# Router logits out of the normalised rows and the head outputs, in column strips, instead of out of the new rows

## The reference

```python
# x (4, 2048, 512); ctx (4, 77, 384); 16 heads of 32; 8 experts, top 2, 1024 slots each
q = layernorm(x) @ Wq + bq;  k = ctx @ Wk + bk;  v = ctx @ Wv + bv
x = x + softmax(clip(q k^T / sqrt(32))) v @ Wo + bo
n = layernorm(x)
dot = n @ expert_embeddings.T                    # the logits, (8192, 8)
weights = softmax over the top 2 of dot          # the others are 0
ones = (weights > 0); keep those whose running count per expert is <= 1024
tokens = the kept rows of n, per expert          # (8, 1024, 512)
out = relu(tokens @ first_linear[e].T) @ second_linear[e].T
final = x + scatter_add(out * weight)
```

## Time and profile before

| | |
|---|---|
| median of 3 runs | 1450.96 us |
| the profiled execution | 1453.71 us |
| its span, first to last instruction | 1451.9 us |
| busy: TensorE matmul | 1318.1 us (91%) |
| VectorE | 990.7 us (68%) |
| ScalarE | 811.4 us (56%) |
| GpSimd | 718.6 us (49%) |
| granted TensorE clock, mean | 0.96 of full |

### The profile page before, as it was taken

One profiled execution on the slowest core, in us unless ns is written; L12 is line 12 of the kernel. 1 busy time (PEld: TensorE's weight loads), 2 busy tenths in 40 slices (PEclk: granted clock), 3 DMA queues, 4 the chain that ended last, 5 costly groups with the idle time before them and its releaser, 6 DMA issues.

```text
span 1451.9 us, 30528 instructions
## 1 busy us (share of the span) xinstructions
PE 1318.1 (91%) x12267; PEld 778.8 (54%) x12330; DVE 990.7 (68%) x1808; ACT 811.4 (56%) x1336; POOL 718.6 (49%) x717
## 2 busy tenths in 40 slices
PE   7648999988999899998648999999999999999996
PEld 3436777766676666765436444444444444444442
DVE  8768898999989997899875545455454545455421
ACT  4558888866998889987455504334251413334110
POOL 3287878775778678876413333241513224241301
PEclk9869999999999999999878999999999999999998
DMA  6147898966898767787514665655646465564401
GB/s 195 52 104 184 207 247 213 235 175 169 182 225 192 186 153 188 169 227 175 158 56 141 182 162 159 160 152 128 190 115 178 143 152 176 146 146 120 106 15 44
DMA packets 319575, 228.89 MB, mean 158 GB/s; under 512 B 253305, under 2 KB 253689, under 8 KB 319434
## 3 DMA queue, kind: packets, MB, share of 16 engines
q1 hardware_dynamic: 304074, 176.28, 48.8%
q0 software_dynamic: 15360, 50.66, 12.0%
HBM read 118.98 MB, written 50.86 MB: 117 GB/s over the span
## 4 chain that ended last, share of the span: by engine, by line
PE 70%; DVE 13%; POOL 6%; issue 4%; ACT 3%; SPq 2%; DMA 1%; DVEq 0%; POOLq 0%; ACTq 0%
PE ps L1213 23%; PE ps L1199 23%; PE ps L1099 8%; PE ps L1029 6%; PE ps L1080 3%; PE ps L1116 2%; POOL sd L542 2%; PE ps L1013 2%; DVE ps L1435 1%; DVE sm L1464 1%; DVE x L1486 1%; PE ps L1052 1%; POOL ph L548 1%; PE ps L1002 1%; POOL qT L524 1%
## 5 line engine op out<-in xcount | busy, mean ns | idle before, releaser
L1199 PE MATMUL ps<-xT,w1s 128*128 128x512 f16 (+1 forms) x1632 | 336.0, 368 | 1.9 <-DVE xT L1729 1.5
L1213 PE MATMUL ps<-w2s,hT 128*128 128x512 f16 x1536 | 332.8, 379 | 0.0
L849 ACT ACTIVATE hT<-ps 128x512 f16<-128x512 f32 (+1 forms) x136 | 77.8, 572 | 355.7 <-PE ps L1199 355.7
L1199 PEld LDWEIGHTS ps<-xT,w1s 128*128 128x128 f16 x1632 | 160.5, 98 | 175.2 <-issue 1.9
L1213 PEld LDWEIGHTS ps<-w2s,hT 128*128 128x128 f16 x1536 | 150.2, 98 | 181.3
L593 POOL DMA_INDIRECT out_dram<-ys,idx x64 | 71.4, 1116 | 278.7 <-DVE ys L1769 274.5
L542 POOL TENSOR_TENSOR sd<-sd,rr 128x1232 f32<-128x1232 f32 x64 | 144.2, 2253 | 125.3 <-ACT rr L750 125.3
L1029 PE MATMUL ps<-xnT,wqh 128*128 128x256 f16 x1536 | 196.7, 280 | 5.5 <-ACT partq L732 5.3
L1099 PE MATMUL ps<-woh,oT 128*128 128x512 f16 x768 | 183.4, 389 | 9.6 <-POOL oT L530 3.8
L1759 DVE SCALAR_TENSOR_TENSOR hT<-ps,hT 128x512 f16<-128x512 f32 (+1 forms) x136 | 88.6, 658 | 138.1 <-ACT hT L849 138.0
L1769 DVE SCALAR_TENSOR_TENSOR ys<-ps,gs,og 128x512 f32<-128x512 f32 x64 | 48.0, 751 | 189.7 <-PE ps L1213 189.7
(11 more groups left out here) (206 smaller groups left out, 2003.3 us busy)
## 6 DMA issues: line engine op xcount, KB each, us to landing
xr<-x SPq DMA_DIRECT2D x64, 256.0 KB, 3.7
xrow_dram<-x SPq DMA_DIRECT2D x64, 256.0 KB, 3.6
out_dram<-x SPq DMA_DIRECT2D x64, 256.0 KB, 4.3
stage<-w1T SPq DMA_DIRECT2D x8, 2048.0 KB, 9.6
stage<-w2T SPq DMA_DIRECT2D x8, 2048.0 KB, 8.5
xt<-x SPq DMA_DIRECT2D x59, 256.0 KB, 3.3
xs<-x SPq DMA_DIRECT2D x56, 256.0 KB, 4.1
wqf<-wq SPq DMA_DIRECT2D x1, 1024.0 KB, 7.0
```

The costliest lines, as they stand in the source:

```text
L1199: ins = pe.matmul(hb[z][:, 0:wide], w1s[e % 2][:, a, k, ic * P:(ic + 1) * P], xT[:, 4 * b + k, cols], start=(k == 0 and i == 0), stop=(k = ...
L1213: ins = pe.matmul(yb[z][:, :], hT[:, a, k, s * P:(s + 1) * P], w2s[e % 2][:, b, k, :], start=(k == 0 and i == 0), stop=(k == 7 and i == 2))
```

## The change

The new row is x1 = x + co * (oT Wo + ...) + bo, so its logits are a sum of three parts: the logits of x, those of the head outputs, and a constant. The first part comes from the normalised rows `xnT` times the expert columns, divided by the row's first norm. (The row's mean drops out, since the expert columns are centred.) The second comes from `oT` times Wo times the expert columns, a 512 by 8 matrix that is made once (`expert_mm`, from a turned copy of Wo that is loaded beside it). Both sets of expert columns are split in hi and lo, side by side in 16 of 32 columns.

- **TensorE**: `t2` and `logits` are gone. New are `xe_mm(G)` and `oe_mm(G)`, once per pair of tiles each: 32 fp16 products, with 32 expert columns as the weights in one column strip of the array, and 64 columns (32 rows of each of the two tiles) that move. The eight products of a strip stand one after the other, then the next strip's. `xe_mm` stands between the first `q_mm` and `pv_mm` in even iterations, `oe_mm` before `o_mm` in odd ones. Ahead of the loop the sum over the expert columns moves in front of `q_mm(0, 0)`; `xe_mm(0)` and `expert_mm` are new.
- **VectorE**: `xe_out` and `oe_out` turn the 128 by 64 result in blocks of 32 by 32, from PSUM to SBUF, once per pair each. `routing` loses its copy, runs the norm's three operations first, then the six operations of `logits(R)` in four steps. Ahead of the loop: a maximum and a scale of the expert columns, their split, and (at h = -5) that of the product with Wo.
- **ScalarE**: `t2_copy` is gone (64 copies of 128 by 512).
- **GpSimd**: a third `all_max`, of the expert columns, between the second and the third `q_lo` of pair 0, and two memsets.
- **SyncE**: the expert columns are loaded earlier; a turned Wo (1 MB) and bo are loaded after Wo.
- `pick`, `put`, `lg` and others lie in other places in SBUF.

```diff
@@ gpsimd, ahead of the loop
+            pool.memset(exs[:, :, :], 0.0)
+            pool.memset(ews[:, :, :], 0.0)
...
             all_max(0, 1)
             all_max(1, 2)
             q_lo(0, 0)
             q_lo(0, 1)
+            all_max(8, 3)
             q_lo(0, 2)
             q_lo(0, 3)
@@ scalar
-                act.wait_ge(S["t2"], t + 1)
-                act.copy(x1T[:, :, :].rearrange("p k n -> p (k n)"), bT[:, :]).then_inc(S["x1T"], 1)
@@ tensor
-                for k in range(4):
-                    ins = pe.transpose(bT[:, k * P:(k + 1) * P], x1[:, t % XO, k * P:(k + 1) * P], identf[:, :])
...
-                for k in range(4):
-                    ins = pe.matmul(bM[:, E * j:E * (j + 1)], x1T[:, k, :], embc[:, k, :], start=(k == 0),
-                                    stop=(k == 3))
...
+            def strips(out, w, src):
+                for i in range(4):
+                    for k in range(4):
+                        for a in range(2):
+                            rows = src(a, k).rearrange("p (j n) -> p j n", j=TG)[:, :, DH * i:DH * (i + 1)]
+                            ins = pe.matmul(out[DH * i:DH * (i + 1), :], w[:, k, :], rows,
+                                            start=(k == 0 and a == 0), stop=(k == 3 and a == 1),
+                                            tile_position=(0, DH * i))
+                return ins
+            def xe_mm(G):
+                pe.wait_ge(S["xTl"], TG * G + TG)
+                if free["M"]:
+                    pe.wait_ge(*free["M"])
+                strips(bM[:, 0:64], exs, lambda a, k: xnT[:, G % 2, 4 * a + k, :]).then_inc(S["xm"], 1)
+            def oe_mm(G):
+                pe.wait_ge(S["olo"], 2 * G + 2)
+                if free["M"]:
+                    pe.wait_ge(*free["M"])
+                strips(bM[:, 64:128], ews, lambda a, g: oT[:, G % 2, a, g, :]).then_inc(S["om"], 1)
+            def expert_mm():
+                for g in range(4):
+                    for k in range(4):
+                        pe.matmul(bM[:, 320 + E * g:320 + E * (g + 1)], wot[:, k, g * P:(g + 1) * P], embc[:, k, :],
+                                  start=(k == 0), stop=(k == 3))
@@ the loop of tensor
+                if half == 1:
+                    oe_mm(G)
                 o_mm(h)
                 if H:
                     invert(H)
                 tx(h + 11)
                 q_mm(Q, 2 * part)
+                if part == 1:
+                    xe_mm(Q)
                 pv_mm(G + 1, half)
                 s_mm(h + 7)
-                t2(h)
                 q_mm(Q, 2 * part + 1)
-                logits(h)
+                if h == -6:
+                    expert_mm()
@@ vector
+            def xe_out(G):
+                    dve.wait_ge(S["xm"], G + 1)
+                    dve.transpose(xe[:, t:t + TG, :].rearrange("p j c -> p (j c)"), bM[:, 0:64]).then_inc(S["xe"], 1)
+            def logits(R):
+                then(dve.reciprocal(den[:, 0:n], rs1[:, t0:t1]))
+                then(dve.tensor_tensor(lg[:, 0:n, :], mine[0][:, :, 0:E], mine[0][:, :, E:2 * E], ALU.add))
+                yield
+                then(dve.tensor_tensor(m8[:, 0:n, :], mine[1][:, :, 0:E], mine[1][:, :, E:2 * E], ALU.add))
...
+                k = then(dve.tensor_tensor(lg[:, 0:n, :], lg[:, 0:n, :],
+                                           den[:, 0:n].unsqueeze(2).to_broadcast([P, n, E]), ALU.mult))
+                yield
...
+                k = then(dve.scalar_tensor_tensor(lg[:, 0:n, :], m8[:, 0:n, :], scr[:, 37:38], lg[:, 0:n, :],
+                                                  ALU.mult, ALU.add))
+                yield
...
+                then(dve.tensor_tensor(lg[:, 0:n, :], lg[:, 0:n, :], be[:, :].unsqueeze(1).to_broadcast([P, n, E]),
+                                       ALU.add))
+                yield
             def routing(R):
-                dve.wait_ge(S["lg"], t1)
-                dve.tensor_copy(lg[:, 0:n, :], bM[:, 0:n * E].rearrange("p (j e) -> p j e", j=n)
-                                ).then_inc(S["lgc"], 1)
-                yield
+                yield from second_norms(R)
+                yield from logits(R)
@@ the loop of vector (the same in the last iterations for oe_out)
                 residual(h)
+                if h % 2:
+                    oe_out(h // 2)
...
+                if h % 2 == 0:
+                    xe_out((h + 9) // 2)
```

More of the change, by code:

```diff
@@ L82, in alternate, with xattn_moe @@
                 gens.remove(gen)
-def xattn_moe(nc, x, ctxT, wq, bq, wk, bk, wv, bv, wo, bo, embT, w1T, w2T, out, xrow):
+def xattn_moe(nc, x, ctxT, wq, bq, wk, bk, wv, bv, wo, bo, woT, boT, embT, w1T, w2T, out, xrow):
     ctx = ExitStack()
@@ L200, in xattn_moe @@
         vsh = sb("vsh", [P, 2, B, D], F16)
+        pick = sb("pick", [P, 4, TG, 2, P], F16)
+        put = sb("put", [P, 4, TG, 2, 64], F16)
+        oe = sb("oe", [P, 16, 32], F32)
+        assert place[0] <= early1
         place[0] = oT_at
@@ L626, in gpsimd @@
                 if h == -7:
-                    all_max(3, 3)
+                    all_max(3, 4)
                 if h == -6:
-                    all_max(2, 4)
+                    all_max(2, 5)
                 if h == -3:
@@ L1014, in t2 @@
-                ins.then_inc(S["t2"], 1)
-                free["T"] = S["x1T"], t + 1
+                    ins = pe.matmul(bM[:, 352:360], bob[:, k:k + 1].to_broadcast([P, P]), embc[:, k, :],
+                                    start=(k == 0), stop=(k == 3))
+                ins.then_inc(S["ew"], 1)
+                free["M"] = S["ewl"], 2
             def q_mm(G, g):
@@ L1226, in tensor @@
             values_mm(1)
-            q_mm(0, 0)
-            q_mm(0, 1)
             pe.wait_ge(S["l_em"], 16)
@@ L1233, in tensor @@
             ins.then_inc(S["early"], 1)
+            q_mm(0, 0)
+            q_mm(0, 1)
             q_mm(0, 2)
@@ L1237, in tensor @@
             tx(2)
+            xe_mm(0)
             values_mm(3)
@@ L1260, in tensor @@
                 pv_mm(G + 1, half, 1)
+                if half == 1:
+                    oe_mm(G)
                 o_mm(h)
                 s_mm(h + 7)
-                if h > TAIL:
-                    logits(h - 1)
                 if H:
                     invert(H)
-                t2(h)
                 if h == 59:
@@ L1277, in tensor @@
                     rank(3)
-            logits(T - 1)
             invert([24, 25, 26])
@@ L2015, in layout @@
         "bo": c(g["L0_xattn_bo"]),
+        "woT": c(g["L0_xattn_Wo"].reshape(4, 4, DH, D).transpose(3, 1, 0, 2).reshape(D, D)),
+        "boT": c(g["L0_xattn_bo"].reshape(4, P).T),
         "embT": c(g["L0_ffn_expert_embeddings"].T),
```

152 lines of the change are left out of this document (91 added, 61 removed).

## The result

The changed kernel takes 1480.74 us in the median (1477.84 to 1482.75, four runs), the kernel before, run beside it, 1451.61 (1449.02 to 1458.66, four runs). The ratio is 1.0194, with a 95% interval of 1.0169 to 1.0220. I had forecast 1455 and at most 1468. The direction was right; the size, 4 us, was not: the profiled executions differ by 25.2 us (spans 1451.9 and 1477.1).

What follows compares the result with a forecast made beforehand. TensorE was taken to set the pace in calm stretches, VectorE in the routing tiles. Relief -8, VectorE +6, head +7 and last tiles -1.5, with a rounded half for bank M, gave +4: 1455 us, range 1443 to 1468.

Steps and rivals of the forecast that it cites:

- Head, +7.0: Ahead of the loop: the fourth `q_lo` ends 7.0 us later, with no slack behind it; bounds 0 to 8.
- the detour: GpSimd ahead of the loop: `all_max(8)` between `q_lo`s adds one change of code each way, about 6 us.
- Products, 0.030: TensorE's new 64-column products: 0.030 us each as in `invert`, 1.92 us per pair, weight loads hidden.
- the rival's estimate of 0.06: TensorE's weight loads don't hide: 0.06 us per new product, a pair loses 1.4 us, 1487 us in all; chance 0.08.
- TensorE's relief, -8: Calm tiles: TensorE sets the pace, each pair gains 0.54 us; 17.5 pairs give -9.4, taken as -8 us.
- VectorE, +6: VectorE in the loop: block transposes +4 and the new logits operations +2, together +6 us.
- the turnings, +4: VectorE's block transposes from PSUM, 0.2 us per tile: nothing in calm tiles, +4 us in 24 routing tiles.
- the sum of 11: Six `logits(R)` operations on VectorE: 3.7 us per large span, 11 us for three, before deductions.
- 4.4 for `dd`: VectorE's `dd` moves three steps back, behind its waits for GpSimd: 2.2 us off in each of two spans.
- The +2 of this sub-sum: VectorE's logits operations: 11, less 1 for the copy, 3.5 for the third span and 4.4 for `dd`.
- Waits on bank M, half a microsecond: A rounded half microsecond added to the sum for what stands behind the new waits on bank M.
- Last tiles, -1.5: Last four tiles: -3.5 us without `t2`, +1.1 for `oe_mm(31)`, +0.8 for the last span's routing.

Runs made afterwards that it cites:

- Both edits together: Changed kernel with `all_max(8)` directly behind `all_max(1)` and the eight expert-column mean products behind `q_mm(0, 1)`: 1470.94 us, ratio 1.0141.
- the two runs: Kernel before without `t2`, its copy and most of `logits`: 1439.94 us; changed kernel with 4 of 32 products per `xe_mm` and `oe_mm`: 1470.67 us.
- the step ahead of `s_recip`: Changed kernel with five `logits(R)` operations in one step before `s_recip`, the `oe` sum earlier as one reduction: 1467.99 us, ratio 1.0092.
- mended: Changed kernel with five logits operations before `s_recip`, `all_max(8)` and mean products moved, last `oe_mm` and its turning before `rank(3)`: 1461.95 us, ratio 1.0056.

## Why the forecast was right in sign and wrong in size

Two steps failed: the relief on TensorE, booked one for one, and the price of the routing steps on VectorE, put at +2 and measured at 16.7. Both errors made the change look cheaper than it was; the right sign rests on the head's 7 us.

- **Head, +7.0: right in size** (7.8), and the steps named are there: `q_lo(0, 2)` at 45.61 behind 6.77 us of "issue", switches of 5.90 and 6.77. Both edits together take 6.2 of the 7.7 away. But the detour, to which I gave 6 of the 7 us, gave back only 2.2 when it went alone, in a profile with a dip of the clock; so the number is borne out and its split is not. Profiles of one head differ by up to 4 us, which I had not in the range.
- **Products, 0.030: cheaper**, 0.023 and 0.020, and their loads hide. Of the rival's estimate of 0.06, which the Trainium skill's rule (TensorE: Matmul & The Clock Gate, Part 3) would give for strips that share their rows, this case shows nothing.
- **TensorE's relief, -8: the first step that failed.** I read 97.5% busy as "sets the pace" and booked the relief one for one. Measured: 0.16 per microsecond in the calm tiles. An estimate from the two runs, over all 64 tiles: the removal returns 13.1, the new products take 8.6 of it again (7.5 for 28 of 32), which leaves -4.5 where I had -8. The changed kernel's calm tiles 0 to 16 gained nothing at all (+0.4).
- **VectorE, +6: the step that failed most.** Its parts: the turnings, +4, were worth about 0.7 (doubled). The six operations I had priced at 3.7 us per span; they took 5.5. From the sum of 11 I took off 3.5 because the third span's would be absorbed, and 4.4 for `dd`. The third span's first tiles lost 3.6 like the others. `dd` and the subtraction ahead of it took 10.0 us with their waits before (5.7 + 2.5 + 1.8) and 9.2 after (5.2 + 3.8 + 0.2): 0.8 and not 4.4. The +2 of this sub-sum was measured at 16.7, by leaving five of the operations out with three of their steps. The operations' own time is 16.6 us in the three large spans, the copy that went 0.8; the turning of `xe` and TensorE's `oe_mm` stand behind them. But that the two numbers agree is not the whole account. From tile 16 to 63 VectorE's operations other than turnings take 457.8 us before, 470.5 in the changed kernel and 456.5 with the step ahead of `s_recip`, and this last one still loses 7.5 us there. So held operations explain about half of the 16.3, and the other half is not traced to a cause.
- **Waits on bank M, half a microsecond: undersized.** `oe_mm` sat idle 17.4 us ahead of its products and `xe_mm` 9.9; taking 9.7 of it away gave 7 from tile 16 to 63, part of which is the same time as in the point before.
- **Last tiles, -1.5: half right.** Tiles 60 to 62 gain 3.4 us. Tile 63 loses 4.2 and not 1.1: `oe_mm(31)` waits 2.12 us for bank M until `ranking(3)` has read it, and it and the `o_mm` behind it run at a lower clock (0.50 granted from 757 to 761 us). That `o_mm` takes 4.87 us, against 3.92 in the kernel before and 2.75 at full clock. TensorE's timeline:

```profile
757.76 1.22 PE L1013 MATMUL ps<-oT,ews 128*32 128x64 f16 x32 [2.12 <-DVE pm L1691]
758.92 0.61 PE L1135 MATMUL ps<-bo,onesb 128*128 128x512 bf16 x1
759.32 4.87 PE L1140 MATMUL ps<-woh,oT 128*128 128x512 f16 x12
```

What stays open: why mended still loses some 10 us between tiles 35 and 57, operation by operation; what the half of the loop's loss is that stays when VectorE's operations take no longer in all than before; and whether a schedule exists in which none of VectorE's routing steps meets GpSimd's long ones. That the shift from one held operation to another explains it was seen in rows, not shown by a run.

## What to carry to other kernels

An engine that is busy 97% of a stretch need not set its pace: before booking relief, take the work out once and see what a microsecond returns (here 0.16). Price a small operation by where it stands, not by its mean: the same addition took 0.23 or 2.25 us, and which depends on what the neighbour engine has just begun; moving it moves everything behind it too. When a new result shares a bank, a queue or a semaphore with old work, list who stands behind it at each of its turns, the last one above all.

## What the runs showed of the hardware

- Some VectorE operations on SBUF operands that start while GpSimd works on a large fp32 tensor end only with GpSimd's: 2.25 us for 128 elements, 2.47 for 16 (`dd`). This was not only so with two inputs, as my expectations had it: `TENSOR_SCALAR` on 16 int32 took 1.55 and 0.16. Others never were held: in the changed kernel the view of single lines gives the shortest, median and longest of each (ns),

```profile
L1491 DVE TENSOR_REDUCE sm<-sd x128: 744/782/789, 72.9 to 724.9; 128x8 f32<-128x616 f32 x128
...
L1519 DVE BATCH_NORM_STATS2 st6b<-x x64: 650/680/696, 132.8 to 765.1; 128x6 f32<-128x512 f32 x64
...
L1621 DVE MAX8 m<-lg x64: 128/150/170, 299.1 to 771.6; 128x8 f32<-128x8 f32 x64
...
L1557 DVE STREAM_TRANSPOSE xe<-ps x32: 216/228/241, 43.1 to 687.4; 128x64 f32<-128x64 f32 x32
```

  so in this kernel the reduction of one input, the statistics, `MAX8` and the block transpose out of PSUM were never the longer for standing beside GpSimd.
- 64-column products in one column strip after another: 0.020 to 0.023 us each; strips taking turns: 0.010. The weight loads hid in both: a quarter of a 256-column product of `q_mm`, 0.109 us in the earlier trace rows, is 0.027.
- GpSimd's change between a reduction and ordinary work cost 5.87 to 7.75 us all six times between 31 and 76 us of the changed kernel, in either direction, and not only the first.
- Two profiles of the same program up to that point had granted clocks of 0.89 and 1.00 between 20 and 50 us, and tile 0 came 4 us apart. A third, different up to there only in the order of the strips' products, had 0.89 too and came 1.7 us behind the one with 1.00.
